# A decoder block on one core: a separate program for the first batch, ahead of the loop

## The reference, cut to what matters

```
x = layernorm(x + attention(x))            # 16 heads of 32, causal, softmax, Wq Wk Wv Wo with biases
x = layernorm(x + wkv(decay, first, x, ctx))   # a recurrence over the 256 tokens, per channel
x = layernorm(x + gated_attention(x))      # W_qkv; one head's k and v is picked per token by W_gate
return x
```

## Time and profile before

| | us |
|---|---|
| median of 3 runs | 1743.57 |
| the profiled execution's own time | 1743.83 |
| its span, first to last instruction | 1742.0 |
| busy: PE / DVE / ACT / POOL | 1454.9 / 1106.0 / 647.9 / 396.5 |
| mean granted TensorE clock | 0.954 of 2.4 GHz |
| moved over DMA | 118.24 MB |

### The profile page before, as it was taken

How to read it: one execution, slowest core, us unless ns; L and a number is a source line. 1 busy time by engine, 2 the same in 40 slices (tenths; PEclk the granted TensorE clock), 3 DMA queues, 4 the chain that set the end, 5 groups by cost and what they waited for, 6 DMA issues and landing times.

```text
span 1742.0 us, 29718 instructions
## 1 busy us (share of the span) xinstructions
PE 1454.9 (84%) x9792; PEld 1141.6 (66%) x9792; DVE 1106.0 (63%) x2267; ACT 647.9 (37%) x1456; POOL 396.5 (23%) x541
## 2 busy tenths in 40 slices
PE   4667989889898988989898898988898898889755
PEld 4546667767676767766677776666677676667443
DVE  3246585766758575665857567685856667585644
ACT  3224252533425343342534334252524434252412
POOL 1013140221304032230403123041312304141220
PEclk8668999999999999999999999999999999999879
DMA  5223232231323222132322213232321313232010
GB/s 141 72 79 84 64 83 71 56 82 46 85 55 91 67 62 68 46 85 55 91 67 65 65 46 86 54 91 67 70 70 44 99 34 91 67 82 59 13 49 13
DMA packets 63282, 118.24 MB, mean 68 GB/s; under 512 B 14480, under 2 KB 32912, under 8 KB 63248
## 3 DMA queue, kind: packets, MB, share of 16 engines
q1 hardware_dynamic: 63248, 117.80, 26.7%
...
## 4 chain that ended last, share of the span: by engine, by line
PE 54%; DVE 25%; issue 8%; ACT 7%; DMA 3%; POOL 1%; SPq 1%; DVEq 1%; ACTq 0%; POOLq 0%
PE pp L411 12%; PE pp L413 10%; PE pp L412 10%; PE po L509 5%; DVE neg_max L1155 4%; PE sq L457 2%; PE po L513 2%; DVE w_key L1230 2%; DMA q_stack<-max_rows 2%; DVE w_max L1225 2%; PE po L523 2%; DVE w_val L1321 2%; DVE o_tok L1180 2%; ACT prob L875 1%; PE sq L436 1%
## 5 line engine op out<-in xcount | busy, mean ns | idle before, releaser
L875 ACT ACTIVATE prob<-sk 128x512 f32<-128x512 f32 x384 | 215.2, 594 | 439.0 <-PE sk L436 438.7
L1155 DVE TENSOR_REDUCE neg_max<-sq 128x2 f32<-128x512 f32 (+1 forms) x384 | 249.6, 677 | 47.4 <-PE sq L436 39.5
L411 PE MATMUL pp<-xt_hi,w_hi 128*128 128x256 f32 x768 | 234.4, 305 | 30.9 <-DVE w_lo L1142 14.2
L412 PE MATMUL pp<-xt_lo,w_hi 128*128 128x256 f32 x768 | 221.1, 288 | 0.0
L413 PE MATMUL pp<-xt_hi,w_lo 128*128 128x256 f32 x768 | 221.0, 288 | 0.0
L411 PE MATMUL pp<-w_hi,xt_hi 128*128 128x512 f32 x384 | 168.2, 438 | 26.4 <-DVE w_val L1321 22.1
L411 PEld LDWEIGHTS pp<-xt_hi,w_hi 128*128 128x128 f32 x768 | 151.1, 197 | 40.3 <-issue 25.7
L412 PE MATMUL pp<-w_lo,xt_hi 128*128 128x512 f32 x384 | 157.0, 409 | 0.0
L413 PE MATMUL pp<-w_hi,xt_lo 128*128 128x512 f32 x384 | 156.8, 408 | 0.0
L412 PEld LDWEIGHTS pp<-xt_lo,w_hi 128*128 128x128 f32 x768 | 151.3, 197 | 0.7
L413 PEld LDWEIGHTS pp<-xt_hi,w_lo 128*128 128x128 f32 x768 | 150.9, 197 | 0.0
...
## 6 DMA issues: line engine op xcount, KB each, us to landing
q_stack<-q_hi SPq DMA_DIRECT2D x256, 128.0 KB, 2.3
q_stack<-q_lo SPq DMA_DIRECT2D x128, 128.0 KB, 2.3
k_stack<-k_hi SPq DMA_DIRECT2D x128, 128.0 KB, 2.3
...
```

Of the source, the lines that this page charges most:

```text
L411: T.matmul(out, lh, rh, start=(c == 0), stop=False, skip_group_check=True)
L412: T.matmul(out, lh, rl, start=False, stop=False, skip_group_check=True)
L875: A.activation(dst, sk[n % 2][:], ACT.Exp, scale=SCALE).then_inc(s_exp, 1)
L1155: V.tensor_reduce(dst, src, AX.X, ALU.max, negate=True).then_inc(s_max, 1)
```

## The change

The first iteration gets a program of its own, `opening()`, on SP, PE, ACT and DVE, in place of what stood ahead of `iteration(0)` and of `iteration(0)` itself. Iteration 1 and all later ones keep their program, but for the banks of batch 1's projections, which fall in the opening, and one added step on POOL.

- `w_raw` is laid over `w_lo`: a raw chunk lands where its low part goes, and the subtraction is in place. No slot and no wait for one is left.
- SP's first issue is `x_raw`; W_Q, W_K and half of W_V follow, with the small constants between. W_O, W_FQ, W_FK, W_FV are four DMAs of 1 MB issued by ACT.
- x of batch 0 is split in four chunks, the low part on DVE (before: on POOL, whole), and PE waits chunk by chunk (`each`).
- Batch 0's jobs 0 to 5 write `pp, pw, pp, pw, po, pp`; batch 1's `pp, po, pp, po, pp, pp`. A job waits for the reading of the job two before.
- In the first attention `sq` of group g + 2 and the maxima of g + 1 are issued beside `sk` of group g; the turned output is split one group later. The order of uses of the bank `pt` changes (`A_M_FIRST`, `A_OT_FIRST`).
- The output projection starts its first three chunks before the last group's output is split.
- The low parts of W_FQ and W_FK move from DVE to POOL's iteration 0, that of W_FV to POOL's iteration 1; W_O's stays on DVE, in halves. The row of ones in `k_stack` is all set by POOL.

Cut to its core (indentation reduced):

```
+A_M_FIRST, A_OT_FIRST = (0, 1, 2, 4), (3, 5, 6, 7)
...
-  w_lo = sb("w_lo", [P, NW, CC, D], f32r)
+  w_lo, w_raw = overlaid("w_lo_region", NW * CC * D * 4, ("w_lo", [P, NW, CC, D], f32r, 0),
+         ("w_raw", [P, NW, CC, D], f32, 0))
...
+  def bank_of(b, job):
+if first_batch(b):
+  return (pp, pw, pp, pw, po, pp)[job]
+if isinstance(b, int) and b == 1:
+  return (pp, po, pp, po, pp, pp)[job]
...
-      wait(sp, w_split_lo, n - 3)
-      sp.dma_start(slot(n), weights_d[w, n % CC]).then_inc(load_w[n % 4], 16)
+def load_weight(w, *chunks):
+  for c in chunks or range(CC):
+    sp.dma_start(raw(w, c), weights_d[w, c]).then_inc(load_w[w][c], 16)
...
+def opening():
+  load_xr_of(0, a_stk, 0)
+  load_weight(W_Q)
+  sp.dma_start(ch_bias[:], ch_bias_d).then_inc(load_c, 16)
+  load_weight(W_K)
+  sp.dma_start(decay[:], decay_d).then_inc(load_c, 16)
+  sp.dma_start(first[:], first_d).then_inc(load_c, 16)
+  sp.dma_start(gate, gate_d.rearrange("(c p) h -> p c h", p=P)).then_inc(load_c, 16)
+  load_weight(W_V, 0, 1)
+  q_stacks(0, PA_JOBS, PA_Q, pa_free, range(1), None, 0, a_stk)
+  load_weight(W_V, 2, 3)
+  q_stacks(0, None, None, None, range(1, 2), None, 0, a_stk)
+  k_stacks(0, range(1))
+  q_stacks(0, None, None, None, range(2, 3), None, 0, a_stk)
+  k_stacks(0, range(1, 2))
+  max_a(0, 0)
+  q_stacks(0, None, None, None, range(3, 4), None, 0, a_stk)
+  k_stacks(0, range(2, 3))
+  max_a(0, 1)
+  k_stacks(0, range(3, 4))
+  sp.dma_start(bo_row[:], row_bias_d).then_inc(load_b, 16)
+  max_a(0, 2)
+  load_x(0)
+  max_a(0, 3)
+  load_xr_of(1, a_stk, 96)
+  load_ctx(0, 0)
+  load_ctx(0, 1)
+  q_stacks(1, PA_JOBS, PA_Q, pa_free, range(NG), None, 0, a_stk)
+  load_ctx(0, 2)
+  load_ctx(0, 3)
+  k_stacks(1, range(2))
+  max_a(1, 0)
+  k_stacks(1, range(2, 3))
...
+  each = None
+  if first_batch(b):
+    def each(c):
+      if job == PA_Q and c < CC - 1:
+        pe.wait_ge(x0_lo, c + 1)
+      if job == PA_WO and c == CC - 1:
+        pe.wait_ge(a_free, A_JOBS * (b + 1))
+      pe.wait_ge(w_split_lo, CC * (W_Q, W_K, W_V, W_O)[job // 2] + c + 1)
+      if job == PA_Q and c == CC - 1:
+        pe.wait_ge(xt_ready, 1)
+    if job == PA_WO:
+      pe.wait_ge(a_free, A_JOBS * b + out_job(b, NG - 2) + 1)
+    elif PA_K <= job < PA_V:
+      pe.wait_ge(pa_free, job - 1)
+    elif job == PA_V + 1:
+      pe.wait_ge(pa_free, PA_K + 2)
+    elif job > PA_WO:
+      pe.wait_ge(pa_free, PA_JOBS * b + job)
...
+    if isinstance(b, int) and b == 1 and PA_Q < job <= PA_V:
+      pe.wait_ge(pa_free, PA_JOBS * b + job - 1)
+    elif job != PA_WO:
...
+def opening():
+  pe.wait_ge(consts, CONSTS)
+  for job in range(PA_WO):
+    project_a(0, job)
+  sq_a(0, 0, 0, 1, 2)
+  max_a(0, 0)
+  sq_a(0, 1, 0, 1, 2)
+  pe.wait_ge(w_ones, 1)
+  for g in range(NG):
+    sk_a(0, g, 0, 1)
+    if g:
+      turn_a(0, g - 1)
+    if g + 1 < NG:
+      max_a(0, g + 1)
+    if g + 2 < NG:
+      sq_a(0, g + 2, 0, 1)
+    sk_a(0, g, 2)
+    if g:
+      out_transpose(0, g - 1)
+    if g + 2 < NG:
+      sq_a(0, g + 2, 2)
+    if g == 0:
+      pe.wait_ge(pa_free, values_done(0))
+    values_a(0, g)
+  turn_a(0, NG - 1)
+  out_transpose(0, NG - 1)
+  project_a(0, PA_WO)
+  project_a(0, PA_WO + 1)
+  project_a(1, PA_Q)
+  x1_transpose(0, 0)
+  project_a(1, PA_Q + 1)
+  x1_transpose(0, 1)
+  project_a(1, PA_K)
+  project_a(1, PA_K + 1)
+  project_a(1, PA_V)
+  pe.wait_ge(a_max, TILES)
+  sq_a(1, 0, 0, 1, 2)
+  max_a(1, 0)
+  pe.wait_ge(a_exp, TILES)
+  sk_a(1, 0, 0, 1)
+  y_transpose(0, 0)
...
+def load_weight(w):
+  act.dma_start(w_raw[:, w, :, :], weights_d[w].rearrange("c p d -> p c d")).then_inc(load_w[w][0], 16)
+def opening():
+  act.wait_ge(load_xr, 16)
+  for c in range(CC):
+    A.activation(xt_hi[:, c, :], x_raw[:, c, :], ACT.Copy)\
+      .then_inc(x0_hi if c < CC - 1 else xt_hi_ready, 1)
+  split_hi(W_Q)
+  act.wait_ge(load_c, 16 * 4)
+  split_hi(W_K, 0, 1)
+  qk_hi(0, PA_Q)
+  split_hi(W_K, 2, 3)
+  qk_hi(0, PA_Q + 1)
+  split_hi(W_V, 0, 1)
+  qk_hi(0, PA_K)
+  split_hi(W_V, 2, 3)
+  qk_hi(0, PA_K + 1)
+  A.activation(gate_hi[:], gate, ACT.Copy).then_inc(gate_split, 1)
+  A.activation(decay[:], decay[:], ACT.Exp).then_inc(act_once, 1)
+  act.wait_ge(act_once, 1)
+  A.activation(decay[:], decay[:], ACT.Copy, scale=-1.0).then_inc(act_once, 1)
+  value_out(0, 0)
+  value_out(0, 1)
+  row_hi_a(0, 0)
+  load_weight(W_O)
+  exps_a(0, 0, 0, 1)
+  row_hi_a(0, 1)
+  exps_a(0, 0, 2)
+  copy_a(0, 0)
+  load_weight(W_FQ)
+  exps_a(0, 1, 0, 1)
+  row_hi_a(0, 2)
+  exps_a(0, 1, 2)
+  out_hi(0, 0)
+  split_hi(W_O, 0, 1)
+  copy_a(0, 1)
+  load_weight(W_FK)
+  exps_a(0, 2, 0, 1)
+  row_hi_a(0, 3)
+  exps_a(0, 2, 2)
+  out_hi(0, 1)
+  split_hi(W_O, 2, 3)
+  copy_a(0, 2)
+  load_weight(W_FV)
+  exps_a(0, 3, 0, 1)
+  exps_a(0, 3, 2)
+  out_hi(0, 2)
+  copy_a(0, 3)
+  x_split_hi(1)
+  out_hi(0, 3)
+  split_hi(W_FQ)
+  split_hi(W_FK)
+  qk_hi(1, PA_Q)
+  act.wait_ge(dve_once, 3)
+  carry_exps(0, 0)
+  qk_hi(1, PA_Q + 1)
+  carry_exps(0, 1)
+  now_exps(0, 0)
+  now_exps(0, 1)
+  qk_hi(1, PA_K)
+  carry_exps(0, 2)
+  now_exps(0, 2)
+  qk_hi(1, PA_K + 1)
+  carry_exps(0, 3)
+  now_exps(0, 3)
+  value_out(1, 0)
+  row_hi_a(1, 0, a_mrow[NG - 1], 32)
+  exps_a(1, 0, 0, 1)
+  split_hi(W_FV)
...
+def opening():
+  cha = Chain(dve, dve_a, A_LINKS, 0)
+  for c in range(CC):
+    if c < CC - 1:
+      dve.wait_ge(x0_hi, c + 1)
+    else:
+      dve.wait_ge(xt_hi_ready, 1)
+    V.tensor_tensor(xt_lo[:, c, :], x_raw[:, c, :], xt_hi[:, c, :].bitcast(f32), ALU.subtract)\
+      .then_inc(x0_lo if c < CC - 1 else xt_ready, 1)
+  split_lo(W_Q)
+  dve.wait_ge(consts, CONSTS)
+  split_lo(W_K, 0, 1)
+  qk_lo(0, PA_Q)
+  split_lo(W_K, 2, 3)
+  qk_lo(0, PA_Q + 1)
+  split_lo(W_V, 0, 1)
+  qk_lo(0, PA_K)
+  split_lo(W_V, 2, 3)
+  qk_lo(0, PA_K + 1)
+  dve.wait_ge(gate_split, 1)
+  V.tensor_tensor(gate_lo[:], gate, gate_hi[:].bitcast(f32), ALU.subtract)
+  dve.wait_ge(act_once, 2)
+  V.tensor_tensor(now_cap[:], first[:], decay[:], ALU.add).then_inc(dve_once, 1)
+  dve.wait_ge(dve_once, 2)
+  V.tensor_scalar(now_cap[:], now_cap[:], -1.0, NOW_HIGH, ALU.mult, ALU.add).then_inc(dve_once, 1)
+  maxima_a(0, 0)
+  rows_a(0, 0)
+  maxima_a(0, 1)
+  rows_a(0, 1)
+  maxima_a(0, 2, 0, 1)
+  maxima_a(0, 2, 2)
+  normalise_a(cha, 0, 0)
+  rows_a(0, 2)
+  maxima_a(0, 3, 0, 1)
+  out_lo(0, 0)
+  maxima_a(0, 3, 2)
+  split_lo(W_O, 0, 1)
+  normalise_a(cha, 0, 1)
+  rows_a(0, 3)
+  out_lo(0, 1)
+  split_lo(W_O, 2, 3)
+  normalise_a(cha, 0, 2)
+  out_lo(0, 2)
+  normalise_a(cha, 0, 3)
+  out_lo(0, 3)
+  first_residual(0, 0)
+  first_residual(0, 1)
+  first_stats(cha, 0)
+  cha.close()
+  ln_apply(0, 0, xa, xa, x1_ready)
+  qk_lo(1, PA_Q)
+  recurrence_start(0, 0)
+  recurrence_start(0, 1)
+  qk_lo(1, PA_Q + 1)
+  sums(0, 0)
+  sums(0, 1)
+  recurrence_start(0, 2)
+  qk_lo(1, PA_K)
+  divide(0, 0)
+  qk_lo(1, PA_K + 1)
+  divide(0, 1)
+  recurrence_start(0, 3)
+  sums(0, 2)
+  maxima_a(1, 0, 0, 1)
+  maxima_a(1, 0, 2)
+  rows_a(1, 0)
+  sums(0, 3)
+  divide(0, 2)
+  second_residual(0, 0)
...
+G.memset(k_stack[3 * HD:3 * HD + 2, :, :].bitcast(f32), 1.0).then_inc(w_ones, 1)
...
+def split_lo(w):
+  for c in range(CC):
+    pool.wait_ge(w_split_hi, CC * w + c + 1)
+    G.tensor_tensor(w_lo[:, w, c, :], raw(w, c), w_hi[:, w, c, :].bitcast(f32),
+            ALU.subtract).then_inc(w_split_late, 1)
 def iteration(t, prev, nxt):
   if prev:
     inverse_std(t - 1, 1)
+  else:
+    pool.wait_ge(load_b, 16)
+  if isinstance(t, int) and t == 1:
+    split_lo(W_FV)
   add_bo(t)
   if nxt:
     x_split_lo(t + 1)
+  if not prev:
+    split_lo(W_FQ)
   inverse_std(t, 0)
+  if not prev:
+    split_lo(W_FK)
```

More of the change, by code:

```diff
@@ L274, in stack_max @@
                     if part:
-                        wait(sp, s_free, jobs * b + job[g] + 1)
+                        wait(sp, s_free, job + 1)
                     row = 3 * HD + part
@@ L346, in iteration @@
                     max_a(t, 3)
-                    if not prev:
-                        load_weights(W_FV)
                 if prev:
@@ L404, in _, with products @@
         def _(pe):
-            def products(out, lhs, rhs, middle=None, at=CC // 2):
+            def products(out, lhs, rhs, middle=None, at=CC // 2, each=None):
                 for c in range(CC):
+                    if each is not None:
+                        each(c)
                     if middle is not None and c == at:
@@ L594, in project_a @@
+                    mm = tokens_out(bank_of(b, job), W_V, job - PA_V, middle=middle, at=at, each=each)
                 else:
-                    mm = tokens_out(pp, W_O, job - PA_WO, k_hi, k_lo)
+                    mm = tokens_out(pp, W_O, job - PA_WO, k_hi, k_lo, each=each)
                 mm.then_inc(pa_job, 1)
@@ L605, in project_f @@
                 if job < PF_K:
-                    mm = channels_out(W_FQ, job - PF_Q, middle)
+                    mm = channels_out(pp, W_FQ, job - PF_Q, middle)
                 elif job < PF_V:
```

228 lines of the change are left out of this document (74 added, 154 removed).

## The result

Four runs each on one chip: 1699.64 us median (1695.39 to 1702.16) against 1741.65 (1739.19 to 1743.73). The ratio is 0.9755, 95% interval 0.9734 to 0.9775: 42 us less. The profiled execution took 1698.18 us, its span is 1696.3, at a mean clock of 0.969.

What follows compares the result with a forecast made beforehand. It took PE's waits and lowered clock in the first 154.8 us as the bound. Output projection at 64.5 plus 40 puts iteration 1 at 104.5, 50.3 off, less 1 is 49: 1743.8 - 49 = 1695 us, range 1685 to 1712.

Steps and rivals of the forecast that it cites:

- Stage A: Start to first sq of batch 0, 48.1 us before: first sq predicted at 28, bounds 26.5 and 31.
- late next: Batch 0's projections: W_V's second half, landed near 22.8, then split on ACT ahead of the last qk_hi, ending near 24.5.
- Stage B: First sq to first output projection, 64.3 us before: 36.5 predicted, ending at 64.5, bounds 57 and 78.
- The 3 us for loads next to stacking DMAs: First attention: ACT's four 1 MB loads delay stacking DMAs by 0.8 to 2.3 each, 3 to 9; 3 taken.
- 5.2 per group: First attention: PE's own work per group at clock 1.00, against 8.6 at 0.61; 6.3 taken at about 0.8.
- The rule: First attention: loads from another engine's queue use the same 16 DMA engines; by it the stage is 6 us longer.
- the ring of the maxima: First attention, per group: turned maxima to sk, 3.2 us; with PE's issues and ACT's exps a limit of 5.0.
- Stage C: First output projection to iteration 1, 42.4 us before: 40 predicted, bounds 38 and 46, iteration 1 at 104.5.
- POOL in the way: Rival, chance 0.10: POOL's low parts of W_FK and W_FV hold up DVE, 8 x 1.29 = 10 us, 1705.
- Behind it: Iteration 1 onward: ACT's high part of W_FV ahead of the third exp tile costs 1 us; tail and loop 0.
- Slower, by the loop's clock: Rival, chance 0.02: each of 13 loop passes settles 3.9 us above 100.6, clock about 0.96, undoing the 49 gained.
- The ideal case: Rival, chance 0.12: all attention groups at 5.2 us, no load in the way, 6 + 4.4 + 1.5 better, about 1685.

Runs made afterwards that it cites:

- the run with W_V ahead: Changed kernel, but SP issues W_V's second half with its first half, not behind the first q stacks; 1695.4 us.
- the run with one bank: Changed kernel, but all projections of batches 0 and 1 write the one bank pp again, each waiting for the previous reading; 1715.44 us, ratio 0.9844.
- the run with W_FK later: Changed kernel, but POOL makes W_FK's low part in iteration 1, ahead of W_FV's; 1695.5 us.

## Why the prediction was right, and where it was off

It said 1695, 1685 to 1712, faster with 0.96; measured 1699.6, against a time of before 2 us lower in the paired runs. Forecast 49 us off, measured 42. That the time lies 5 us from the forecast is in part luck: below, a main cause is missing from its reasons, and the loop alone moves a run by as much.

- **Stage A.** First projection at 7.9, came at 7.1, as x was there at 4.4, ahead of the earliest bound of 4.6; first sq at 28, came at 29.0 and 28.0. The two waits named as "late next", W_V's second half and the last reading of k, were there (1.32, and k_hi at 24.33), and the run with W_V ahead confirms them. The run with one bank confirms what the banks are worth, and that a good two fifths of it are the clock (5.3 of 12.6).
- **Stage B.** 36.5 said, 38.3 and 38.5 measured. The 3 us for loads next to stacking DMAs were the right size: 2.8 between first sq and first sk alone, by W_O's load. Clock 0.8 said, 0.78 read; but at 0.8 the working's own 5.2 per group makes 6.5, not 6.3, and at 0.78 6.7, so four groups 26.7 for 25.2: 1.5 of the 1.8 that were missing. The sign of being wrong, waits of over 2 us for rows in each group, did not show: 2.87, none, none, 1.76. The rule that the prediction takes from the Trainium skill, page "DMA: Bandwidth & Descriptors", section "Issuing engines are not separate DMA queues", agrees with the traces: the load issued by ACT at 11.6 us held nothing up, issued at 32.3 it made SP's rows late by 2.8, and issued at 38.2 PE waited 6.70 for SP's k stack. But the reason given for the stage was incomplete. The prediction put its old length down to low parts between divide and output split; all splits of three matrices put back, high parts too, are 4 of 26, and the v job that moved 4. Loading by slots, 18, was only in the sum because PE's own work and the ring of the maxima were costed afresh, from below. The low parts do matter, but as what the slots waited for. The number was right for a cause not named.
- **Stage C.** 40 said, 41.9 and 40.5 measured; its parts less well. To the end of the second residual it gained 1.9 where 1 was said. From there to the first sq of batch 1 it takes 25.3 and 23.9, for 24.1 before, where 2.3 less for the banks and 1.5 more for POOL make 23.3. From that sq to iteration 1 it takes 9.0 for 8.85, where 0.7 less was said: the v job that left had covered the wait for the rows, 0.84 before and 2.95 now. That ACT would read the last k job only behind the recurrence's third chunk (k job done at 91.6, k_hi from 95.36) is not in the working, which had looked at SP's order alone.
- **POOL in the way.** This rival, given 0.10 and 10 us, happened in part: two norms at 2.89 and 2.65 for 1.00, 3.5 us in all, of which the sum had 1.5. The step that failed is the sentence that what DVE does meanwhile "reads PSUM on one side, mostly". The norm has one input, in SBUF, and was held up all the same. The Trainium skill, page "SBUF — State Buffer", section "Who interferes with whom", has that case beside the one that was cited: tensor_scalar can run in a mode that uses both ports and then contends with GpSimd. By that reading both norms could be expected to wait; the traces agree (2.89, 2.65 and 2.88 beside a POOL subtraction, 1.00 without), and the run with W_FK later shows it by taking the neighbour away.
- **Behind it.** 1 us said, 4.2 measured at the first store. The term was mis-sized: it counted ACT's high part of W_FV, not that iteration 1 would be entered at the lower clock level (0.97 for that iteration, 1.00 before) and with W_FV's split on the second norm.
- **Slower, by the loop's clock.** Did not happen; but the two lengths of a pass are that mechanism in small, and it acts on both kernels: 7 and 5 long ones of 12.
- **Slips in its sums.** The ideal case's parts, 6 + 4.4 + 1.5, make 1683, not about 1685. The chances of the cases that end faster add to 0.97, not 0.96. Neither changes the forecast.

Still open: why a pass is long or short, how much of the 4.2 is the clock alone, and what the slots would cost without the splits in the attention. No kernel here changes the clock by itself.
